# Expert masks of the last three token groups multiplied on VectorE instead of GpSimd, with a fourth mask buffer

## The reference, cut to what matters

```python
x = x + 0.5 * ffn(layernorm(x), ...)
x = x + attention(layernorm(x), ...)
x = x + 0.5 * ffn(layernorm(x), ...)

def ffn(x):
    scores = sigmoid(x @ gate_w.T + lb_bias)
    topw, topi = top_k(scores, 2)              # 2 of 8 experts
    topw = topw / (topw.sum(-1, keepdims=True) + 1e-08)
    for e in range(8):
        m = topi == e
        sel = m.any(axis=-1)
        wmean = (topw * m).sum() / max(m.sum(), 1)
        y = mlp(x, gate_w[e], up_w[e], down_w[e])   # silu(x g) * (x u) d, 64 wide
        out = out + where(sel[:, None], y * wmean, 0)
    return out + mlp(x, shared_gate_w, shared_up_w, shared_down_w)   # 128 wide
```

## Time and profile before

| what | value |
|---|---|
| median of 3 runs | 749.88 us (749.0 to 750.06) |
| time of the profiled execution | 747.74 us |
| its span in the trace | 746.0 us |
| PE busy | 699.1 us (94%) |
| DVE busy | 582.6 us (78%) |
| ACT busy | 403.4 us (54%) |
| POOL busy | 112.5 us (15%) |
| first FFN, up stage to the first `wds` matmul | 0 to 95 us |
| its down stage, with the preparation of attention | 95 to about 184 us |
| attention and the output projection | to about 616 us |
| second FFN, first `wds` matmul | 706.6 us |

### The profile page before, as it was taken

The page is one execution under the profiler, slowest core; times in us unless marked ns, Lnnn a source line. Parts: engine busy times, 40 slices in busy tenths (PEclk is TensorE's granted clock), DMA queues, the critical chain, the costliest instruction groups (busy, mean ns, idle before and its releaser), DMA issues.

```text
span 746.0 us, 15875 instructions
## 1 busy us (share of the span) xinstructions
PE 699.1 (94%) x5880; PEld 367.9 (49%) x5880; DVE 582.6 (78%) x1921; ACT 403.4 (54%) x579; POOL 112.5 (15%) x122
## 2 busy tenths in 40 slices
PE   4999998976999999999999999999999886999998
PEld 3554487842344444444444444444444274554498
DVE  5987458787999999999999999999999047766311
ACT  2353333132667777776777677777767832343300
POOL 2111962110000000000000000000000002102960
PEclk9999999975799999999999999999999997999999
DMA  7013633442110101001100101110010000005751
GB/s 215 0 17 67 107 57 97 143 151 77 31 39 25 28 26 39 20 20 38 36 23 20 39 21 29 29 37 21 20 38 1 2 1 0 2 0 89 104 95 57
DMA packets 47249, 34.69 MB, mean 47 GB/s; under 512 B 13106, under 2 KB 46514, under 8 KB 47172
## 3 DMA queue, kind: packets, MB, share of 16 engines
q1 hardware_dynamic: 46596, 33.60, 19.3%
q10 hardware_dynamic: 576, 0.08, 0.1%
HBM read 23.01 MB, written 10.39 MB: 45 GB/s over the span
## 4 chain that ended last, share of the span: by engine, by line
PE 53%; DVE 13%; issue 11%; ACT 2%; DVEq 0%; ACTq 0%
PE ps L1017 49%; DVE mx L902 8%; PE ps L1022 4%; DVE mx L895 1%; ACT h_all L623 1%; DVE h_all L895 1%; DVE xn L704 1%; DVE stats L692 0%; DVE wb L922 0%; DVE mm_ L919 0%; DVE sg L837 0%; ACT osb L612 0%; DVE idle L893 0%; DVEq L132 0%; DVE mv L696 0%
## 5 line engine op out<-in xcount | busy, mean ns | idle before, releaser
L623 ACT ACTIVATE h_all<-ps 128x1024 f32<-128x1024 f32 (+3 forms) x384 | 291.3, 811 | 112.1 <-PE ps L1017 108.9
L902 DVE TENSOR_REDUCE mx<-ps 128x1 f32<-128x512 f32 (+2 forms) x352 | 223.0, 681 | 9.2 <-PE ps L1017 6.7
L1017 PE MATMUL ps<-ks,xnT_all 57*128 57x512 bf16 (+3 forms) x768 | 179.1, 336 | 14.7 <-DVE mx L895 6.4
L1017 PE MATMUL ps<-h_all,vb 128*32 128x512 f32 (+3 forms) x1536 | 163.6, 499 | 0.6 <-ACT osb L612 0.6
L1017 PE MATMUL ps<-xnT_all,ks 59*128 59x512 bf16 (+3 forms) x768 | 158.9, 332 | 3.3 <-ACT h_all L623 3.1
L895 DVE CUSTOM_DVE_ANT_0 h_all<-ps,mask_w 128x384 bf16<-128x384 f32 (+1 forms) x256 | 149.3, 618 | 2.2 <-issue 0.5
L1017 PEld LDWEIGHTS ps<-ks,xnT_all 57*128 57x128 bf16 x768 | 56.4, 94 | 142.9 <-DVE mx L895 64.9
L1017 PE MATMUL ps<-cb 64*128 64x64 bf16 (+3 forms) x1216 | 112.9, 215 | 0.0
L716 DVE TENSOR_TENSOR h_all<-ps,sg 128x512 f32<-128x512 f32 x80 | 55.2, 690 | 55.5 <-PE ps L1017 53.8
L562 ACT ACTIVATE sg<-ps 128x512 f32<-128x512 f32 x80 | 47.8, 597 | 85.9 <-PE ps L1017 85.7
L1017 PEld LDWEIGHTS ps<-cb 64*128 64x128 bf16 x1216 | 80.1, 96 | 17.3 <-issue 1.0
(11 more groups left out here) (118 smaller groups left out, 539.5 us busy)
## 6 DMA issues: line engine op xcount, KB each, us to landing
xnT_all<-q_scr SPq DMA_DIRECT2D x64, 96.0 KB
attn<-sel_scr SPq DMA_DIRECT2D x12, 256.0 KB, 7.3
mask_second<-sel_scr SPq DMA_DIRECT2D x12, 256.0 KB, 8.3
q_scr<-qp SPq DMA_DIRECT2D x8, 384.0 KB
ks<-k_scr SPq DMA_DIRECT2D x64, 48.0 KB
x<-in_x SPq DMA_DIRECT2D x8, 256.0 KB, 6.1
yT<-sel_scr SPq DMA_DIRECT2D x8, 256.0 KB, 9.3
q_scr<-qp SPq DMA_DIRECT2D x8, 256.0 KB
```

The source lines that it names most:

```text
L623: act.activation(pr[:, (NSTEP * i + s) % PR_BUFS, p:HPG:SLOTS, lo:HALF], ps[:, b:b + 2, lo:HALF], ACT.Exp)\
L902: dve.tensor_reduce(m, src, AX.X, V.max).then_inc(a_out, 1)
L1017: return pe.matmul(o, l, r, start=start, stop=stop, skip_group_check=True)
```

## The change

POOL multiplies the masks of groups 0 to 4 only (`POOL_MASKS`), ahead of all its `rsqrt` of the down stage. The 12 tiles of groups 5 to 7 (`DVE_MASKS`) are multiplied by DVE, which raises a semaphore of its own, `hd`: two masks behind each of the last four products of the up stage (groups 5 and 6), and two in the body of the down stage for c = 0 and for c = 1 (group 7), behind the statistics and ahead of `ln_apply`. Both FFNs do so. PE's `down` waits for `hm` for groups 0 to 4 and for `hd` for 5 to 7. A fourth mask buffer shares memory with `v_all`, so a mask is loaded once POOL is done with the group four back, not three back. SP's program keeps its order.

```diff
-MASK_BUFS, MASK_PARTS = 3, MT
-AHEAD = 6
+MASK_BUFS = 4
+POOL_MASKS = 5
+DVE_MASKS = [(c, i) for c in range(POOL_MASKS, GROUPS) for i in range(MT)]
...
+        mask_fourth = v_all.rearrange("p u t d -> p (u t d)").bitcast(BF16).rearrange("p (m n) -> p m n", m=MT)
+        expert_mask = (mask_first, mask_second, mask_third, mask_fourth)
...
             def load_mask(f, c):
 
-                after(sp, f.hm, MASK_PARTS * (c - MASK_BUFS + 1))
+                after(sp, f.hm, MT * (c - MASK_BUFS + 1))
...
-            for c in range(AHEAD):
+            for c in range(POOL_MASKS):
                 mask_hidden(f1, 0, c)
             for c in range(GROUPS):
                 rsqrt(c, c % 2, f1.ve2, f1.xn2, f1.rs2)
-                if AHEAD + c < GROUPS:
-                    mask_hidden(f1, 0, AHEAD + c)
...
-            for c in range(GROUPS):
+            for c in range(POOL_MASKS):
                 mask_hidden(f2, 1, c)
...
+            def mask_tiles(f, n, some):
+
+                for c, i in some:
+                    b = c % MASK_BUFS
+                    dve.wait_ge(f.h, TILE_ORDER.index((c, i)) + 1)
+                    dve.wait_ge(s_mask[b], mask_uses(n, c))
+                    dve.tensor_tensor(h_all[:, c, i, :], h_all[:, c, i, :], expert_mask[b][:, i, :], V.mult)\
+                       .then_inc(f.hd, 1)
...
                     hidden(k)
                     if k == TOPS_AT:
                         scale_down()
+                    first = 2 * (k - len(TILE_ORDER) + MT)
+                    if first >= 0:
+                        mask_tiles(f, 0 if first_ffn else 1, DVE_MASKS[first:first + 2])
...
                         ln_stats(c, par, ch, f.ve2)
                         early_maxima(early(c, 0))
+                    if c < 2:
+                        mask_tiles(f, 0 if qkv else 1, DVE_MASKS[2 * (MT + c):2 * (MT + c) + 2])
+                    if qkv:
                         ln_apply(c, par, f.rs2, f.Tb, f.xn2)
...
-                    pe.wait_ge(f.hm, MASK_PARTS * (c + 1))
+                    if c < POOL_MASKS:
+                        pe.wait_ge(f.hm, MT * (c + 1))
+                    else:
+                        pe.wait_ge(f.hd, MT * (c - POOL_MASKS + 1))
```

More of the change, by code:

```diff
@@ L101, with mask_uses @@
 assert len(EARLY) == GROUPS
+def mask_uses(n, c):
+    b = c % MASK_BUFS
+    return 32 * (n * (GROUPS // MASK_BUFS) + c // MASK_BUFS + 1)
 def early(c, k):
@@ L119 @@
 W0_STEP = 5
-FFN_SEMS = ("ve", "rs", "xn", "T", "xA", "gl", "lg", "sig", "sel", "mT", "mk", "md", "hm", "G", "U", "sg", "h", "tot", "tops",
+FFN_SEMS = ("ve", "rs", "xn", "T", "xA", "gl", "lg", "sig", "sel", "mT", "mk", "md", "hm", "hd", "G", "U", "sg", "h", "tot", "tops",
             "wds", "Y", "x", "ch_up", "ch_down", "ve2", "rs2", "xn2", "Tb", "xTb", "Q", "K", "V", "qf",
@@ L264, in macaron @@
             .rearrange("p (m n) -> p m n", m=MT)
-        mask_last = yT.rearrange("p a n -> p (a n)").bitcast(BF16).rearrange("p (m n) -> p m n", m=MT)
-        expert_mask = (mask_first, mask_second, mask_last)
+        mask_third = yT.rearrange("p a n -> p (a n)").bitcast(BF16).rearrange("p (m n) -> p m n", m=MT)
+        mask_fourth = v_all.rearrange("p u t d -> p (u t d)").bitcast(BF16).rearrange("p (m n) -> p m n", m=MT)
+        expert_mask = (mask_first, mask_second, mask_third, mask_fourth)
         assert len(expert_mask) == MASK_BUFS
@@ L301, in macaron @@
         s_ks0 = sem("s_ks0")
-        s_mask = [sem("s_mask_first"), sem("s_mask_second"), sem("s_mask_last")]
+        s_mask = [sem("s_mask_first"), sem("s_mask_second"), sem("s_mask_third"), sem("s_mask_fourth")]
         def ffn_sems(n):
@@ L484, in mask_hidden @@
                 b = c % MASK_BUFS
[L485 to L493, removed]
+                for i in range(MT):
+                    pool.wait_ge(f.h, HT * c + 1 + i + 1)
+                    if i == 0:
+                        pool.wait_ge(s_mask[b], mask_uses(n, c))
+                    pool.tensor_tensor(h_all[:, c, i, :], h_all[:, c, i, :], expert_mask[b][:, i, :], ALU.mult)\
+                        .then_inc(f.hm, 1)
             over_groups(lambda c, par, first, last: rsqrt(c, par, f1.ve, f1.xn, f1.rs))
```

## The result

The median after is **756.37 us** (750.04 to 759.8, 8 runs) against 749.56 (747.76 to 750.73, 8 runs) for the kernel before: a ratio of 1.008, 95% interval [1.005, 1.0109]. The change costs 6.8 us by the medians and 6.0 by the ratio.

A forecast was written before the change was run, and what follows sets the result against it. PE was taken as the bound over most of the span, with its own waits the question. Terms -4.0 + 1.2 + 4.2 + 1.8 = +3.2 on 747.74 gave 750.9, and 2.14 more the median 753.1 us; range 748.3 to 757.5.

The forecast's parts named there:

- the signs that the prediction named: Short `ln_apply`, no PE transpose wait, stores and attention 4 us earlier; second FFN: PE waits 4 to 6 us, clock 0.5.
- the second rival: The first FFN's 4.0 us are lost on the way, by a store or first maxima: +7.2, 757.1 us, chance 0.19.
- First FFN, -4.0: Down stage of the first FFN: without POOL's masks in `ln_apply`'s way, the split starts 4.0 us earlier; bounds 0 to 5.6.
- The following steps keep this: After the first FFN's split: the 4.0 us stay gained, as SP's own list sets the pace of the stores.
- looked at below for the second FFN, where it matters: Last tiles of the up stage: two masks, 1.36 us, are not quite hidden per tile; nothing booked for the first FFN.
- Second FFN, last tiles, +1.2: DVE's masks and products end at 712.45, so the addition of group 0 starts 1.2 us late (0 to 3.0).
- PE's `wu` of the last tile may slip too, but that is covered by the next wait: Second FFN's last tile, at 705.72: a slip of PE's matmuls there was claimed covered, with nothing booked for it.
- W: DVE's wait for POOL's group 4 masks in the second FFN's last tiles: between 0 and 3.5 us, taken as 1.75.
- Late mask, +4.2: Second FFN: group 7's mask, loaded behind group 0's store, lands 9.69 us later; PE waits 4.2 us ahead of group 3.
- clock, +1.8: Second FFN, behind PE's wait for the late mask: the clock drops and costs 1.8 us (0 to 3.4).
- the clock holds: First rival: no clock drop in the second FFN and masks hardly meet POOL's: +0.8, 750.7 us, chance 0.18.
- group 7's mask lands in time: Third rival: in the second FFN it lands 5.5 us behind its issue, PE does not wait: -4.0, 745.9 us, chance 0.13.

The follow-up runs named there:

- the square: Four kernels with the change in both FFNs; second FFN's masks between last tiles or behind last product, group 7's load late or ahead: 756.37, 750.6, 752.71, 746.9 us.

## Why the prediction was right, and which term was off

The median of 756.37 us lies in the stated range of 748.3 to 757.5, and the signs that the prediction named appeared, except that attention's first matmul by V was 2.66 us earlier and not 4. But the median lies outside the forecast's own 751.4 to 755.4 and nearest to the second rival's 757.1: the range held it because it was drawn wide enough for that rival, whose cause did little. That part is luck. Most of the difference is one term, the second FFN's last tiles.

**First FFN, -4.0.** The mechanism and the size at the split hold (4.23 us; ACT sets it; no wait at the transpose). "The following steps keep this" cannot be judged from the two traces of before and after, in which 2.66 is left at the first matmul by V. Two traces with the unchanged first FFN differ there by 1.25 us themselves (102.00 and 103.25 behind the first `wds`). The eleven with the change in it lie at 97.2 to 99.9; the means are 3.7 us apart. Measured alone and undisturbed, the first FFN's part gives -3.6 by the medians. Why the landings take differently long from one execution to the next was not tried.

The forecast booked nothing for the last tiles of this FFN ("looked at below for the second FFN, where it matters"). The masks stand between those tiles in eight traces, not counting the run with an input from PSUM; in six of these the masks waited for all of POOL's and PE then waited 1.5 to 2.4 us for a product. The kernel with the first FFN's part alone gains nothing measurable with the masks there and 3.6 us with them behind the last product.

**Second FFN, last tiles, +1.2.** This is the term that was mis-sized: 4.26 in the trace, above its bound of 3.0, and 2.3 to 3.7 in the comparisons. The step that failed is "PE's `wu` of the last tile may slip too, but that is covered by the next wait": the slip sets the end of this stage. DVE had its masks done by 713.03, only 0.58 later than the 712.45 forecast, and then waited 2.48 us for PE. PE's `wds` started 3.57 late, by its own wait of 2.39 and by the low clock behind it, which the step had not counted. The smaller error is the wait for POOL, W. It was taken as half of POOL's remaining work, 1.75, with 3.5 as its bound; the two masks took 5.38 us and not 1.28, which is 4.10 more, since the first waited for all four of POOL's. It showed less in the sum because group 5's mask, forecast to land at 703.2, was there at 702.24.

**Late mask, +4.2, and clock, +1.8.** Measured 4.03 and 1.85; together 5.8 by the medians of the square and 4.0 to 4.9 by its ratios. Loading ahead takes both away, which shows the cause. The 7.3 us that the prediction called the shortest landing is a median; in the four traces in which DVE waits for this load, it landed 9.0 to 9.7 us behind its issue.

**Sum.** -2.7 + 4.26 + 4.03 + 1.85 = +7.4 against the +6.8 of the medians; the forecast had +3.2.

**Rivals.** That the clock holds fell: it dropped behind both waits. That the 4.0 is lost on the way came true for 1.3 us in the two traces at hand, but the means over all traces keep 3.7. That group 7's mask lands in time fell: it came 9.72 us behind the issue, where 5.5 were needed.

**The rule.** The Trainium skill (SBUF — State Buffer, "Who interferes with whom") says that a VectorE instruction with two SBUF inputs and a GpSimd one that reads SBUF exclude each other, and that one with at most one SBUF input, outside the two-port modes, is free of this. The runs agree on both: 5.14 us for two masks with both inputs in SBUF, 1.28 with one in PSUM. With W at 3.5, as for engines strictly in turn, the prediction's sum would have been 1.7 higher, which is nearer to the result; but the traces show turns in only 2 of 13 cases.

## What to carry to other kernels

Before moving work with two SBUF inputs to VectorE, look at what GpSimd does in the same microseconds. Book GpSimd's whole remaining run, not one instruction of it (11 of 13 meetings here), and follow the delay to the engine that waits for VectorE next. Work moved to an in-order engine that carries the critical path must find its data there, so check which transfer it now waits for and what that transfer is queued behind. When a change has a gain and a loss in two stages, apply it to each stage alone: here the first FFN's half, with the masks behind the last product, is 3.6 us faster than before.

## What the runs showed of the hardware that was not expected

A waiting mask on VectorE was passed over by GpSimd's next instructions. In the change's second FFN the first of the two masks alone took from 702.24 to 707.02, past the end of GpSimd's four at 706.47:

```profile
702.24 4.78 DVE L717 TENSOR_TENSOR h_all<-h_all,mask_second 128x512 f32<-128x512 f32 x1
```

In two other meetings the engines alternated, and both slowed (2.66 and 2.46 us for two masks, 5.87 and 5.86 for GpSimd's four).

A wait of PE of 2.39 us was not always followed by the lower clock. In the change's second FFN two `wu` matmuls behind it took 2.08 us, at a granted clock of 0.55; in the first FFN of the kernel with that FFN's part alone, two behind the same wait took 1.13, at 1.00.

The low stretch of the clock at the start of the second FFN has no fixed length, with the same work in it. By the windows of all 13 traces it lasted 10.2 us in three (before among them), 13.6 in seven (the change among them) and 17.1 in three, some of it while PE waits for the transposes. The kernel with the second FFN's masks behind the last product had 10.2 in one execution and 17.1 in another. The shorter one ends 0.80 of the way through this window:

```profile
624.00:626.00 2.00, 2.00 (x11) 0.60 0.00 0
```

The change's execution lost 1.85 us to it against that of before. As the same kernel had both lengths, this is put down to the executions and not to the change; the kernel before has only one trace.
